# A Swin-like block, in chunks of eight windows: MLP layer one and projection as two column halves, and new issue orders

## What is computed

```python
xn = layernorm(xw) * ln_g + ln_b                       # 49 tokens of a window, 96 channels
q, k, v = heads(xn @ qkv_w.T + qkv_b)                  # 12 heads of 8
attn = softmax(q * 8 ** -0.5 @ k.T + bias[head])
seq = x + (attn @ v) @ proj_w.T + proj_b
seq2 = batchnorm(depthwise_conv3x3(seq))
out = seq2 + gelu(seq2 @ w1.T + b1) @ w2.T + b2
```

## Time and profile before

| | |
|---|---|
| median of 3 runs | 3189.77 us (3189.08 to 3205.73) |
| the profiled execution | 3164.1 us |
| its span, first to last instruction | 3162.3 us |
| mean granted TensorE clock | 0.993 |
| busy: PE, DVE, ACT, POOL | 96%, 91%, 88%, 62% |
| chain that ended last | PE 91%, issue 3%, ACT 2%, others 1% or less |

### The profile page before, as it was taken

How to read it: one execution, slowest core, us unless ns; L and a number is a source line. 1 busy time by engine, 2 the same in 40 slices (tenths; PEclk the granted TensorE clock), 3 DMA queues, 4 the chain that set the end, 5 groups by cost and what they waited for, 6 DMA issues and landing times.

```text
span 3162.3 us, 199772 instructions
## 1 busy us (share of the span) xinstructions
PE 3029.4 (96%) x88076; PEld 2105.9 (67%) x88076; DVE 2888.8 (91%) x4908; ACT 2768.5 (88%) x4867; POOL 1956.6 (62%) x2574
## 2 busy tenths in 40 slices
PE   3899999999999999999999999999999999999997
PEld 2666666666766666666666666666666676666663
DVE  4799999999999999999999999999999999999996
ACT  2799999989989999998989999988989999998986
POOL 2566666666666666666666666666666666666664
PEclk9999999999999999999999999999999999999998
DMA  1233333333333333333333333333333333333331
GB/s 40 86 91 96 91 96 94 92 95 91 97 91 94 95 94 95 96 91 95 91 96 94 94 96 94 92 96 91 95 95 93 96 97 93 95 98 91 95 92 41
DMA packets 269922, 288.31 MB, mean 91 GB/s; under 512 B 55651, under 2 KB 252580, under 8 KB 269062
## 3 DMA queue, kind: packets, MB, share of 16 engines
q1 hardware_dynamic: 236294, 198.40, 22.6%
q0 software_dynamic: 32768, 77.14, 7.0%
HBM read 39.34 MB, written 38.54 MB: 25 GB/s over the span
## 4 chain that ended last, share of the span: by engine, by line
PE 91%; issue 3%; ACT 2%; SPq 1%; DMA 1%; DVE 1%; POOL 0%; POOLq 0%; ACTq 0%; DVEq 0%
PE d_ps L255 21%; PE st_ps L299 12%; PE o_ps L345 11%; PE sm_ps L320 10%; PE b_ps L363 7%; PE b_ps L399 6%; PE a_ps L255 4%; PE b_ps L255 4%; PE a_ps L266 3%; PE a_ps L268 3%; PE a_ps L267 3%; PE d_ps L266 1%; PE d_ps L268 1%; PE b_ps L267 1%; PE d_ps L267 1%
## 5 line engine op out<-in xcount | busy, mean ns | idle before, releaser
L764 DVE SCALAR_TENSOR_TENSOR s<-ximg,cols,s 96x392 f32<-96x392 f32 x1792 | 1137.0, 635 | 30.7 <-POOL s L627 3.2
L738 DVE TENSOR_REDUCE mx<-sm_ps 128x12 f16<-128x588 f32 x1024 | 785.0, 767 | 127.7 <-PE sm_ps L320 125.1
L474 ACT ACTIVATE p<-st_ps 128x588 f32<-128x588 f32 x1024 | 672.4, 657 | 179.2 <-PE st_ps L299 176.1
L637 POOL DMA_DIRECT2D ox<-o_sb x1024 | 582.7, 572 | 30.8 <-ACT o_sb L499 17.2
L320 PEld LDWEIGHTS sm_ps<-k_all,q_all 127*49 127x49 f16 x24576 | 460.6, 104 | 171.5 <-issue 76.0
L255 PE MATMUL d_ps<-g,w_s 128*64 128x392 f32 x3072 | 560.2, 500 | 0.0
L299 PEld LDWEIGHTS st_ps<-q_all,k_all 128*49 128x49 f16 x24576 | 435.5, 103 | 157.2 <-issue 107.8
L610 POOL TENSOR_TENSOR s<-ximg,cols 96x392 f32<-96x392 f32 x256 | 216.0, 844 | 520.5 <-DVE y L801 519.9
L299 PE MATMUL st_ps<-q_all,k_all 128*49 128x49 f16 x24576 | 516.1, 186 | 21.4 <-issue 19.3
L320 PE MATMUL sm_ps<-k_all,q_all 127*49 127x49 f16 x24576 | 508.6, 186 | 25.9 <-issue 15.6
L599 POOL TENSOR_TENSOR xl<-xn,xh 96x392 f16<-96x392 f32 x256 | 258.8, 1011 | 273.6 <-ACT xh L555 256.5
(11 more groups left out here) (122 smaller groups left out, 5959.7 us busy)
## 6 DMA issues: line engine op xcount, KB each, us to landing
ox<-o_sb POOLq DMA_DIRECT2D x1024, 73.5 KB
k_all<-kh SPq DMA_DIRECT2D x512, 75.0 KB
q_all<-qh SPq DMA_DIRECT2D x512, 75.0 KB
x_sb<-in_x SPq DMA_DIRECT2D x256, 147.0 KB, 2.4
out<-y SPq DMA_DIRECT2D x256, 147.0 KB, 2.7
q_all<-ql SPq DMA_DIRECT2D x256, 75.0 KB
k_all<-kl SPq DMA_DIRECT2D x256, 75.0 KB
q_all<-mxt SPq DMA_DIRECT2D x256, 9.4 KB, 2.1
```

What stands on the lines that cost most here:

```text
L474: af(p32[:, p, :, :].rearrange("p (b h) n -> p b h n", b=2), st_ps[:, :, 0:HALF].rearrange("p b (h n) -> p b h n", n=TOK), ACT.Exp).then_i ...
L637: nc.gpsimd.dma_start(ox[:, c % 2, x4, :], o_sb[x4::4, c % 2, :, :]).then_inc(o_in[c % 2], 16)
L738: v.tensor_reduce(mx[:, c % 2, 0:HEADS, p].rearrange("p (b h) -> p b h", b=2), sm_ps[:, :, 0:HALF].rearrange("p b (h n) -> p b h n", n=TOK ...
L764: v.scalar_tensor_tensor(acc, image_rows(c, k // 3, k % 3), cw_c[:, k:k + 1], acc, ALU.mult, ALU.add)\
```

## The change

`hidden` goes from `whole_three` to `halves_three`, and takes a_ps for k = 1 and k = 2 (b_ps held k = 2 before). `projection` goes from one matmul of 96 columns a window parity to `halves` over the padded 128. The maxima are transposed over 48 columns (they were padded with zeros to 96). The lists of all five engines are in another order:

```diff
-        mx, mxt = sb("mx", [128, 2, 2 * HEADS, NP], F16), sb("mxt", [HEADS * NP, 2, 2, KP], F16)
+        mx, mxt = sb("mx", [128, 2, HEADS, NP], F16), sb("mxt", [HEADS * NP, 2, 2, KP], F16)
-        mxt_ps = sm_ps[0:2 * HEADS * NP, 0, 0:64].bitcast(F16)
+        mxt_ps = sm_ps[0:HEADS * NP, 0, 0:64].bitcast(F16)
@@ projection
-                    o = b_ps[0:C, 0:CT].rearrange("c (r n w k) -> c w n r k", r=WS, w=2, k=WS)[:, w]
-                    last = mm(o, wp[:, 0:C], ox[:, c % 2, w, :].rearrange("c (n r k) -> c n r k", n=NP, k=WS), start=True, stop=True)
+                    o = b_ps[0:128, 0:CT].rearrange("c (r n w k) -> c w n r k", r=WS, w=2, k=WS)[:, w]
+                    last = halves(o, wp[:, :], ox[:, c % 2, w, :].rearrange("c (n r k) -> c n r k", n=NP, k=WS))
@@ hidden
-            hidden_ps = {0: d_ps, 1: a_ps, 2: b_ps}
+            hidden_ps = {0: d_ps, 1: a_ps, 2: a_ps}
-                whole_three(hidden_ps[k][:, 0:CT], w1_h[:, k * 128:(k + 1) * 128], w1_l[:, k * 128:(k + 1) * 128], sh[:, :], sl[:, :]).then_inc(hid_done[k], 1)
+                    free(pe, (g_done[1], c), (v32_done, c+5), (ql_done, c+6), (g_done[2], c-1))
+                halves_three(hidden_ps[k][:, 0:CT], w1_h[:, k * 128:(k + 1) * 128], w1_l[:, k * 128:(k + 1) * 128], sh[:, :], sl[:, :]).then_inc(hid_done[k], 1)
@@ SP
-                load(s)
-                first_term(k_all, 0, kh, kh_done, s - 3)
+                term(q_all, 2, ql, ql_done, s - 4)
+                term(k_all, 1, kl, kl_done, s - 4)
+                store(s - 12)
+                term(k_all, 0, kh, kh_done, s - 4)
+                maximum_row(s - 5)
+                load(s)
+                first_term(q_all, 0, qh, qh_done, s - 3)
+                term(q_all, 1, qh, qh_done, s - 3)
                 term(k_all, 2, kh, kh_done, s - 3)
...
@@ DVE
+                normalise(s - 5)
                 maxima(s - 2, 2)
                 values_out(s - 2)
                 input_normal(s)
                 maxima(s - 2, 3)
+                tap(s - 6, 2)
+                tap(s - 6, 3)
+                maxima_out(s - 2)
+                tap(s - 6, 4)
                 image_sum(s - 5)
-                tap(s - 6, 2)
-                maxima_out(s - 2)
...
+                tap(s - 6, 5)
                 maxima(s - 1, 0)
                 tap(s - 6, 6)
                 block_out(s - 7)
                 maxima(s - 1, 1)
-                key_low(s)
                 query_low(s)
                 tap(s - 6, 7)
+                key_low(s)
                 tap(s - 6, 8)
-                normalise(s - 4)
@@ POOL
-                first_product(s - 6)
-                second_product(s - 6)
-                image_high(s - 7)
-                image_low(s - 7)
                 add_products(s - 6)
                 to_channels(s - 4)
                 input_low(s)
+                first_product(s - 5)
+                second_product(s - 5)
+                image_high(s - 6)
+                image_low(s - 6)
```

More of the change, by code:

```diff
@@ L422, in second @@
                 wait(pe, g_done[k], c)
-                if k == 0:
+                if k == 1:
                     free(pe, (g_done[0], c), (xn_done, c+7), (y_done, c-1))
-                halves(d_ps[0:128, 0:CT], w2_s[:, k, :], g[:, k, :], start=k == 0, stop=k == 2).then_inc(s_done[k], 1)
+                halves(d_ps[0:128, 0:CT], w2_s[:, k, :], g[:, k, :], start=k == 1, stop=k == 2).then_inc(s_done[k], 1)
             for s in range(STEPS):
-                exp_scores(s - 4, 2)
-                max_scores(s - 3, 3)
-                projection(s - 6)
-                hidden(s - 8, 0)
-                maxima_rows(s - 3)
-                hidden(s - 8, 1)
-                hidden(s - 8, 2)
-                exp_scores(s - 4, 3)
-                max_scores(s - 2, 0)
-                second(s - 8, 0)
-                second(s - 8, 1)
-                second(s - 8, 2)
-                keys(s - 1)
                 max_scores(s - 2, 1)
@@ L443, in _ @@
                 exp_scores(s - 3, 0)
+                keys(s - 1)
+                max_scores(s - 2, 2)
                 centred(s)
-                max_scores(s - 2, 2)
                 exp_scores(s - 3, 1)
@@ L450, in _ @@
                 values(s - 2)
-                values_times_p(s - 3, 0)
-                values_times_p(s - 3, 1)
+                exp_scores(s - 3, 2)
+                projection(s - 5)
+                max_scores(s - 2, 3)
+                hidden(s - 7, 1)
+                hidden(s - 7, 0)
+                maxima_rows(s - 2)
+                values_times_p(s - 3, 1)
+                values_times_p(s - 3, 0)
+                hidden(s - 7, 2)
+                second(s - 7, 1)
+                max_scores(s - 1, 0)
+                exp_scores(s - 3, 3)
+                second(s - 7, 0)
+                second(s - 7, 2)
         @block.scalar
@@ L495, in outputs @@
                     return
-                wait(act, pv_done[1 if half == 0 else 3], c)
+                wait(act, pv_done[0 if half == 0 else 3], c)
                 if half == 0:
```

51 lines of the change are left out of this document (20 added, 31 removed).

## The result

The change makes the kernel slower. Its median is 3240.48 us (3232.30 to 3255.54, 4 executions) against 3191.89 us (3189.08 to 3205.73) of the kernel before beside it: a ratio of 1.015, with a 95% interval of 1.010 to 1.020. Forecast were 3145 us and at most 3212.

The account below looks back on a forecast made before the run. PE was taken to bound the kernel, by its work and by its instruction supply: 11.53 + 0.09 + 0.03 + 0.07 = 11.72 us a step against 11.895, -45 us over the run, so a median of 3145 us, range 3095 to 3212.

Parts of the forecast that it names:

- PE's own work: PE's matmul time per step without stops or waits: 11.53 us after the change, a sum of small terms of -0.03.
- The gelu ahead of the third k = 2: Hidden third k = 2 reuses a_ps, so PE waits for ACT's first gelu: 0.09 us a step, paid in full.
- The transpose's wait: PE's transpose waits for the maxima after max_scores(3) and two thirds: 0.03 us, lying within the gelu's 0.09.
- Near ties: Other meetings with under 0.15 us to spare, including late copies of keys and queries: 0.03 us, bounds 0 and 0.15.
- rival D: Part of the six key and query copies regularly lands late: 0.3 us a step above forecast, 3222 us; chance 0.05.
- The instruction stops: PE running out of instructions at packet edges, every 252: from 0.335 us a step to 0.07, bounds 0 and 0.335.
- The threshold: A window of 252 PE instructions stops PE for what it lacks to 3.3 us: 0.37 a step before, 0.03 after.
- The row that gave 3.7 us: A second stop in the old kernel put the next packet at 3.7 us: 0.80 a step before, 0.19 after.
- A: PE's stops come once in 252 instructions whatever their density: 0.35 us a step, slower, 3217 us; chance 0.15.
- B: No change within 0.5%: PE's stops fall by half to 0.17, ties cost 0.15 us a step, 3201 us; chance 0.15.
- C: Faster by more: values' way into the score block free, gelu in time, stops vanish: 11.47 a step, 3081 us; chance 0.10.

Follow-up runs that it names:

- e10: The changed kernel with p and v of the value products in 16-bit floats, 618 instructions a step: 3108.57 us, 0.969 of the kernel before.
- e9: The changed kernel making the variance twice and the first pair of second-layer halves twice: 3471.89 us, 1.082 of the kernel before.
- e5: The kernel before with p and v in 16-bit floats, 592 instructions a step: 3028.88 us, 0.945 of the kernel before.
- e12: The kernel before with 16-bit p and v, as in e5, run again on another chip: 3016.63 us, 0.952 of the kernel before.
- e2: The changed kernel's new order with the old forms (whole thirds, whole projection, 96 columns): 3225.22 us, 1.017 of the kernel before.
- e1: The kernel before in its old order, with the new forms alone (halves, 48 columns): 3215.89 us, 1.014 of the kernel before.
- e3: The changed kernel without the six copies a chunk into q_all and k_all and the waits for them, one execution: 3180.11 us.
- e6: The changed kernel with the six copies issued together, a step earlier than three of them were: 3242.84 us, 1.011 of the kernel before.
- e8: The changed kernel with the second layer in one piece, max_scores(0) and exp_scores(3) ahead of it: 3250.6 us, 1.025 of the kernel before.

## Why the prediction was wrong

By the terms of its sum, against the first profile:

- **PE's own work** held within 0.1. Forecast were 11.53 us and 0.09 of waiting, 11.62; the undisturbed step has 11.60, with nearly none of that waiting, so the match is in part luck. The projection takes 0.69 (1520.61 to 1521.30, forecast 0.70), a third 0.50 (1521.62 to 1522.12, forecast 0.52), the transpose with its change of width 0.17 (1522.66 to 1522.83, forecast 0.06 + 0.09). Against the 11.56 of an undisturbed step before, 11.60 is 0.04 more; by 10th percentiles it fell by 0.07 to 0.08. So this term is near nothing, as forecast, and its sign isn't settled. That the forms alone save 0.31 in the old order, and the new order alone costs 0.36, had escaped me: I priced only the two together.
- **The gelu ahead of the third k = 2**, 0.09: the meeting was there, its price was too high. From the variance's start (1518.93) the first gelu ends after 4.53 us (1522.87 + 0.59), where my chain gave 4.54. The third starts 0.05 behind that end (1523.51), and I had allowed 0.10. Over the steps 34 to 248 this distance is 0.052 in at least half of them, so the gelu does time the third; but PE's way there adds up to 4.55 by percentiles, and the wait is about 0.03. The view of waits shows 2.4 us, because the value products' recorded durations reach over it. In e10, where two value parts on PE's way are 0.2 us shorter each, it is plain, 79 / 255 = 0.31 a step.
- **The transpose's wait** of 0.03 is there in the row of PE's loads that wait for the maxima (245 times), and small on PE itself: in the timeline it starts 0.20 after the product before it (1522.46 to 1522.66), where products are 0.17 apart.
- **Near ties**, 0.03 with an upper bound of 0.15: held where PE itself is asked. Its matmuls waited (15.3 - 6.0) / 255 = 0.04 a step more for the copies, though its loads waited (46 - 9) / 255 = 0.15 more. This was rival D, priced at 0.3 a step, to which I gave 0.05 because the chain of before had DMA at 1%. That share told of the old list only; the new one issues three of the six a step later, and the text said so.
- **The instruction stops are the step that failed.** "If a window stops PE for what it lacks to 3.3 us, the old order loses 0.37 us a step, where 0.335 was measured, and the new one 0.03 ... I take 0.07; the bounds are 0 and the 0.335 of now." Measured: 0.42 to 0.50 in the new order, where the same measure has 0.25 in the old one. The laying out of windows was right: blocks with under 3.3 us of own time fell from 36% to 7%. The threshold was wrong. I had fitted it to one sum, with a rate per window and each window by itself. In the kernel before, 82 of 95 stops do lie in blocks of under 3.3 us, and of the 94 blocks between 3.7 and 4.6 us, 7 were stopped. In the changed kernel 43 of 45 short blocks stop, 33 of 72 between 3.3 and 3.7 us, and 51 of 425 between 3.7 and 4.6 us. These last alone cost 49 of 109 us. "One dense place is as it was, but few starts fall into it": it is `values_times_p(2)` and `(3)`, and the last of them is stopped in one step out of five, for 0.93 us each time. A second dense place I had not seen at all: `exp_scores(3)`, behind the second layer's first pair, is stopped in 24 steps of 215, for 1.2 us each time.

The upper bound was wrong as well: nothing in the rows said that stops could not grow. The row that gave 3.7 us should have been the value for the sum; the 0.19 that it gives is still less than half of what came.

**What took the threshold's place.** In the trace the packets of the instruction queue come one at a time. In each of the fourteen traces of this study the next one starts at least 2.3 us after the last one's end, and at least 3.3 us after its start; a twentieth of the distances from start to start is under 3.4 to 3.7 us, by kernel, and half of them are over 4.1 to 4.8. Packet and edge belong together one to one. A packet starts once PE has crossed an edge, and at a stop PE goes on 1.4 us after that packet has landed (1.2 to 1.7 in nine of ten, in both kernels). In the changed kernel's first profile, PE stopped at 104 of the 106 edges that it reached less than 1.0 us after the landing, at 3 of 20 between 1.0 and 1.2 us, and at 3 of 434 beyond; in the kernel before at 76 of 83, 6 of 39 and 3 of 438 (560 edges each; a shorter gap than 0.4 us is not counted, so these are the edges reached over 0.4 us ahead of the 1.4). That leaves little room for any other cause of these stops.

So what a block must last is no fixed 3.3 us: it is the time from the edge to the landing, and 1.4. The landing came 2.10 us after the edge on average in the kernel before, and 2.45 and 2.32 in the changed one's two profiles: 3.5 us, and 3.7 to 3.9, with a wide spread (1.6 to 3.5 us for the landing, 5th and 95th percentile, in the changed kernel's first). It also depends on the blocks ahead. Where PE crosses less than 3.0 us after the last packet's start, the next one lands 2.65 us later on average; where it crosses more than 3.5 us after it, 1.97 (changed; 2.42 and 1.63 before). So, as I read it, a short block makes the next packet late, and a long one lets the supply catch up. The old list had 41% of blocks over 4.6 us (the second and hidden layers in one piece). The new one spreads the dense parts so evenly that 12% are, and 69% take 3.7 to 4.6 us: it is close to the pace of the packets most of the time.

The runs bear it out from three sides: work without instructions takes two thirds of the stops away (e9, 45% long blocks), fewer instructions take a third to four fifths (e5, e12, and e10 against the changed kernel), and with the old forms, 0.43 us a step more of PE time, the new order has few (e2, 37%). It is not the share of long blocks alone, for e1 has 34% and the most stops; there the short ones, 35% of all, are stopped more often, 102 times instead of 82, and longer. Every kernel with stops over 0.4 has the 26 further instructions a step, 3.8% more packets in hardly more time.

**Sum.** From before to the first profile, in us a step: -0.08 of own work, +0.25 of stops, and +0.17 of all other waits (0.095 before, 0.26 now), 0.34 of the 0.336 measured; these other waits are what is left of a step, so the sum must close. To the second: -0.07 + 0.17 + 0.11 = 0.21 of 0.21. Of the other waits, 0.04 and 0.03 are PE's matmuls behind the copies, about 0.03 those behind DVE (all such rows of PE: 12.4 us before, 19.3 and 19.6 now); the rest stands in no single row. Not settled is how much of the stops the copies cause. Without them the stops fell to 0.33, and the landing came 2.17 us after the edge (e3); with earlier copies only the waits fell, and the landing stayed at 2.46 (e6).

**The rivals.** A had the stops stay at 0.35 and the time at 3217; it named the right direction, for a wrong reason. The Trainium skill's rule behind it (Runtime: NRT & Kernel Launch, "Instruction fetch mechanics"), that the fetching is hidden behind the pace of issue, does not hold in this kernel: PE stops at every fifth edge of a packet (128 of 615 counted), and far less often when work is added between the edges (52 of 626 in e9). D named the copies, at 0.3 a step. PE's matmuls lost 0.04 to them directly; e3, a single execution, puts the copies' whole share, stops included, at some 0.16. No case of mine had the stops grow by more than 0.02, and the range ended 28 us below the median. B and C had fewer stops, and fell with the threshold.

## What to carry to other kernels

Where an engine runs through hundreds of tiny instructions a step, look for stops that recur at a fixed number of instructions (252 recorded ones here); then instruction count and the time between edges are a budget beside the engine's work. Saving PE time with more instructions gained nothing here (halves, 26 more a step), and taking instructions out gave 5% of the time (16-bit products, 96 fewer, with 0.80 us less work and fewer stops). Price such stops by the pace over several packets and keep long blocks for catching up; a threshold fitted to the order of before says little of an order that spreads the work evenly. And after any move of a reader or of a copy, work out the distance from issue to use anew: a share of 1% in the chain before is no argument. Read what a wait costs from the matmuls' row, not from the loads'.

## What the runs showed of the hardware that I had not expected

- One packet of instructions at a time for PE, 3.3 us from start to start at best, though a packet itself takes only 1.0 to 1.2 us. After PE has crossed into a block, the next packet starts 0 to 2.1 us later in the kernel before and 0.6 to 2.6 in the changed one (medians 1.1 and 1.3; 5th and 95th percentile). The landing is the later the shorter ago the last packet started (2.65 against 1.97 us, above). What else this delay depends on was not tried; the state of the other queues and PE's own waits are both possible.
- Halves of 64 columns cost nothing against whole columns (a hidden third takes 0.50 us either way), and save at the borders: from a score block into the halves of the projection there is no piece of 0.09 us (0.32 in e1, 0.41 before), and the transpose over 48 columns ahead of a half takes under 0.02 us from its start to the next start (e1), while ahead of the 32-column products it takes 0.17.
- A change of one block's place by 0.66 us raised the loads' waits for copies by half and doubled those of PE's matmuls (e8), with the copies themselves issued as before.
